# Taking the parts of a projected half right behind its last product, in a Performer-attention kernel on one core

## Chip, cores and metric

The kernel runs on 1 core of one Trainium2 chip. The metric is the device time of one launch in microseconds. The kernel before took 1294.76 us (median of 3 runs, 1294.49 to 1295.84).

## The reference, cut to what matters

The input x is 8 batches x 1024 tokens x 512 features. Per batch there are 16 heads of 32 features and 128 random features.

```python
def feature_map(x, orf):
    proj = x @ orf.T / d_k ** 0.25
    norm = jnp.sum(x * x, axis=-1, keepdims=True) / (2.0 * math.sqrt(d_k))
    return (jnp.exp(proj - norm) + EPS) / math.sqrt(m)
q = feature_map(split(x @ Wq.T + bq), orf)
k = feature_map(split(x @ Wk.T + bk), orf)
v = split(x @ Wv.T + bv)
kv = jnp.einsum('nlm,nld->nmd', k, v)
ksum = jnp.sum(k, axis=1)
out = jnp.einsum('nlm,nmd->nld', q, concat(kv, ksum))
out = out[..., :-1] / out[..., -1:]          # then @ Wo.T + bo
x = layernorm(x + attention(x))
x = layernorm(x + x @ (ternary(weight) * scale).T)
```

## The kernel before, in words

One core works through the 8 batches in order. The 16 heads are taken as 4 groups of 4. Each group has two *units*, an even one for its keys and an odd one for its queries, so a batch has units 0 to 7, and behind them an output stage (projection, layer norm, ternary product, layer norm).

A matrix product with full precision is made of three products of rounded parts: high x high, low x high, high x low. So each projected tile must be split into a high part (rounded copy), a low part (the rest) and, for the norm, a square.

All work is one list, `SCHEDULE`, of small stages. Every engine walks through the same list and does its own share of each stage, in order, with semaphores between the engines. So a stage's place in the list sets, on every engine by itself, what it is queued behind. `unit_stages` (L72) writes the list of a unit. A stage is a tuple of a letter, the batch, the unit and a piece:

- **P** (PE, L951): six products of 128x512 into one PSUM bank, half of one projected half of a unit. A unit has two halves, each of twelve products, (P, half, 0) and (P, half, 1). In unit u the list holds what belongs to unit u+2 (`two`) and the first part of unit u+3 (`three`): `p[0]` is the second part of half 0 of u+2, with its last product; `p[1]` and `p[2]` are half 1 of u+2; `p[3]` is the first part of half 0 of u+3.
- **S** (`s0`, `s1`; ACT, L649 and L651): the high part and the square of a half, both read from PSUM. **L** (`l0`, `l1`; DVE, L816): the low part, which reads PSUM and waits for both of ACT's. Projections have PSUM banks 0 and 1, taken in turn, and a bank is free again when L has read it; PE waits for that before it starts a P in it.
- **Q** (`q0`, `q1`; DVE, L824 and L828): the squares are transposed and summed. **N** (DVE, L834 to L839): the norms. **LIFT** and **NL** (DMAs of the SP and POOL queues): high, low and norms are copied to the stacked operand of the features of unit u+2.
- **F** (0 to 7; PE, L964 for keys and L969 for queries; ACT, L668): the features of unit u, a tile of 128x512 each. PE's product goes to one of three banks, ACT takes the exponential. In a key unit DVE adds the tiles up: tile 1 is added to tile 0 (L777), tiles 2 to 7 one after the other to the total (L780). These are seven additions, called a1 to a7 here.
- **G** (0 to 7; PE, L982): keys times values. Behind tile 7 the total of the additions is multiplied by ones (L991), which waits for a7. G belongs to a group's query unit and stands behind its F 0 and 1. ACT copies the result (L673 to L680).
- **KVT** (PE, L999 and L1000; DVE, L842): the result transposed. **GG** 0 and 1 (PE, L1014): query features times it; it waits for DVE's copy and for the features of its half, and DVE then transposes, sums and inverts the denominators (L850 to L855). **R** 0 and 1 (DVE, L865 and L867): the division.
- **WF** (DVE, L755 and L756): a quarter of the ternary weights, once in the launch, in batch 0.

The waits that the prediction speaks of:

```python
if old is not None:                                   # PE: the bank's last reader
    pe.wait_ge(*old_bank(old))                        # for P: v_plo, counted by L
pe.wait_ge(v_ks.sem, v_ks.nth(b, 7 * u + 7))          # PE, G of tile 7: a7
pe.wait_ge(v_kvc.sem, v_kvc.nth(b, g + 1))            # PE, GG 0: DVE's copy L842
dve.wait_ge(a_p.sem, a_p.nth(b, 2 * (2 * u + h) + 2)) # DVE, L: high part and square
dve.wait_ge(v_ks.sem, v_ks.nth(b, 7 * g + r - 1))     # DVE, L780: the addition before
```

Of the kernel before, what the change touches and what calls it, by code (L numbers as in the profile page):

```python
# [49 lines left out]
NU = 2 * NG  # L50
# [12 lines left out]
def split_at(b, g):  # L63

    return 4 if sums_on_pe(b, g) else 0


def is_key(u):
    return u % 2 == 0


def unit_stages(b, u):  # L72

    g = u // 2

    def later(k):
        n = NU * b + u + k
        return (n // NU, n % NU) if n < NU * B else None

    def project(unit, h, part):  # L80
        return [("P", *unit, h, part)] if unit else []

    def take(kind, unit, h):
        return [(kind, *unit, h)] if unit else []

    def f(*tiles):
        return [("F", b, u, n) for n in tiles]

    def xt(*tiles):
        return [("XT", b + 1, t) for t in tiles] if b + 1 < B else []  # L90

    two, three = later(2), later(3)
    p = [project(two, 0, 1), project(two, 1, 0), project(two, 1, 1), project(three, 0, 0)]
    s0, s1, l0, l1, q0, q1 = (take(kind, two, h) for kind in "SLQ" for h in range(2))
    norm = [("N", *two)] if two else []
    lift = [("LIFT", *two), ("NL", *two)] if two else []
    if is_key(u):
        st = [[("ST", b - 1, t)] if u == 0 and b else [] for t in (TT - 2, TT - 1)]
        half = [("G", b, g, r) for r in range(split_at(b, g))]
        early = [("AG", b, 0, 0), ("AG", b, 1, 0)] if b + 1 == B and u + 2 == NU else []  # L100
        if u == 0:
            seq = f(0, 1) + p[1] + s0 + l0 + f(2, 3) + q0 + st[0] + p[2] + f(4, 5) + half + s1 + l1 + f(6, 7) + q1 + norm + lift
            seq += st[1] + p[3]
        else:
            seq = f(0, 1) + p[0] + f(2, 3) + p[1] + s0 + l0 + f(4, 5) + q0 + half + p[2] + early + f(6, 7) + s1 + l1 + q1 + norm + lift + p[3]
        if u == 0 and b == 0:
            seq += [("WA", 0, k) for k in range(KT)]
        if u == 2 and b == 0:
            seq += [("WF", 0, 1)]
        if u == 2 and 0 < b < B - 1:  # L110
            seq += [("LX", b + 1, t) for t in range(5)]
        return seq
    kv = [("G", b, g, r) for r in range(split_at(b, g), 8)]
    if u < NU - 1:
        seq = p[0] + f(0, 1)
        if u == 1 and b == 0:
            seq += [("WS", 0)]
        if b + 1 == B and u == NU - 3:
            seq += p[1] + s0 + l0 + kv + f(2, 3) + p[2] + f(4, 5) + s1 + q0 + [("KVT", b, g)] + f(6, 7) + l1 + [("GG", b, g, 0)] + q1 + norm + lift
            seq += [("GG", b, g, 1), ("R", b, g, 0)] + [("LR", b, t) for t in range(4)]  # L120
        elif u < NU - 3:
            seq += kv + f(2, 3) + p[1] + [("KVT", b, g)] + s0 + l0 + f(4, 5) + p[2] + f(6, 7) + s1 + q0 + [("GG", b, g, 0)]
            seq += l1 + p[3] + [("R", b, g, 0), ("GG", b, g, 1)] + q1 + norm + lift
        else:
            seq += xt(0) + kv + f(2, 3) + p[1] + [("KVT", b, g)] + s0 + l0 + xt(1, 2) + f(4, 5) + xt(3)
            seq += [("LX", b + 1, t) for t in range(5, TT)] + p[2] + [("GG", b, g, 0), ("R", b, g, 0)] + q0
            seq += s1 + xt(4) + f(6, 7) + xt(5) + l1 + p[3] + xt(6, 7) + [("GG", b, g, 1)] + q1 + norm + lift
            seq += [("LR", b, t) for t in range(4)]
        seq += [("R", b, g, 1)] if b + 1 < B or u < NU - 3 else []
        if u == 1 and b == 0:  # L130
            seq += [("WF", 0, 0)]
        if u == 3 and b == 0:
            seq.insert(seq.index(("L", 0, 5, 0)) + 1, ("WF", 0, 2))
            seq += [("WF", 0, 3)] + [("LX", 1, t) for t in range(5)]
        return seq
    if b + 1 == B:
        seq = [("R", b, g - 1, 1), ("AG", b, 2, 0)] + f(0, 1, 2) + kv + [("AG", b, 0, 1)] + f(3) + [("OK", b, 0, 0)]
        seq += [("KVT", b, g)] + f(4, 5) + [("AG", b, 1, 1), ("AG", b, 2, 1), ("A", b, 0), ("A", b, 1), ("OK", b, 0, 1), ("OK", b, 0, 2)]
        seq += [("GG", b, g, 0), ("R", b, g, 0, 0), ("AG", b, g, 0, 0)] + f(6, 7) + [("OK", b, 1, k) for k in range(3)]
        seq += [("R", b, g, 0, 1), ("AG", b, g, 0, 1), ("OK", b, 0, 3), ("LN", b, 0), ("OK", b, 1, 3), ("LN", b, 1), ("A", b, 2), ("A", b, 3)]  # L140
        seq += [("GG", b, g, 1)] + [("OK", b, 2, k) for k in range(KT)] + [("LN", b, 2), ("Y", b, 0), ("A", b, 4)]
        return seq + [("LR", b, t) for t in range(4, TT)]
    v0 = [("V", b + 1, 0)] if two else []
    seq = p[0] + f(0, 1) + kv + f(2, 3) + p[1] + [("KVT", b, g)] + s0 + l0 + f(4, 5) + [("GG", b, g, 0)] + q0 + [("R", b, g, 0, 0)]
    seq += p[2] + f(6, 7) + s1 + l1 + [("A", b, 0), ("A", b, 1)] + v0 + [("R", b, g, 0, 1), ("GG", b, g, 1)]
    return seq + [("LR", b, t) for t in range(4, TT)]
# [55 lines left out]
for _b in range(B):  # L202
    for _u in range(NU):
        SCHEDULE += unit_stages(_b, _u)
    SCHEDULE += output_stages(_b)
# [879 lines left out]
```

## Time and profile before

| | |
|---|---|
| median of the runs | 1294.76 us |
| profiled execution, its own time | 1293.62 us |
| its span, first to last instruction | 1291.8 us |
| PE busy | 1262.5 us (98%) |
| PE weight load busy | 958.8 us (74%) |
| DVE busy | 940.8 us (73%) |
| ACT busy | 700.6 us (54%) |
| POOL busy | 326.6 us (25%) |

Busy time is the union of the instructions of an engine; matmuls overlap in the record, so a busy PE is not PE at its peak. The granted TensorE clock was 0.999 over the span.

### The profile page before, as it was taken

To read this page: it belongs to the slowest core of one execution; us is meant where nothing else is said; L and a number is where in the kernel's file an instruction comes from. 1 tells how busy PE (TensorE), PEld (TensorE's weight loads), DVE (VectorE), ACT (ScalarE), POOL (GpSimd) and SP (SyncE) were. 2 spreads that over 40 slices of the span, in tenths; PEclk is the share of its full clock that TensorE was granted. 3 is DMA by queue.
4 is the path that set the end of the run, shared out by engine and by line. 5 is a ranking of instruction groups with operands and counts; after the bars stand their busy time and mean duration, and the time that the engine had idled before them with its cause. 6 is when DMAs were issued, how large, how long until landed. Compare 5 with 4: busy or idle time off the path is not lost.

```text
span 1291.8 us, 24909 instructions
## 1 busy us (share of the span) xinstructions
PE 1262.5 (98%) x8626; PEld 958.8 (74%) x8626; DVE 940.8 (73%) x1775; ACT 700.6 (54%) x1403; POOL 326.6 (25%) x617
## 2 busy tenths in 40 slices
PE   9999999999999999999999999999999999999986
PEld 8767788677877678776787768876788767886665
DVE  6588765887658875788757886588865787657766
ACT  5557435574356743567336663367534665446534
POOL 0102342024310243103431034211252022420043
PEclk9999999999999999999999999999999999999999
DMA  6658404783146821567215762258612685036611
GB/s 236 153 125 220 100 33 121 171 195 88 52 110 174 201 61 58 129 171 187 62 58 130 181 169 65 65 132 209 153 44 71 152 208 142 33 87 144 149 58 65
DMA packets 82749, 160.33 MB, mean 124 GB/s; under 512 B 17856, under 2 KB 36416, under 8 KB 82112
## 3 DMA queue, kind: packets, MB, share of 16 engines
q1 hardware_dynamic: 68880, 139.78, 43.4%
q10 hardware_dynamic: 9648, 16.85, 3.4%
q0 software_dynamic: 4096, 2.11, 0.7%
q8 instruction: 69, 1.13, 0.4%
q14 instruction: 56, 0.46, 0.1%
HBM read 39.13 MB, written 16.78 MB: 43 GB/s over the span
## 4 chain that ended last, share of the span: by engine, by line
PE 76%; DVE 10%; issue 5%; ACT 4%; POOL 0%; ACTq 0%; DVEq 0%; POOLq 0%
PE ps L951 21%; PE ps L914 18%; PE ps L1014 7%; PE ps L964 6%; PE ps L982 5%; PE ps L937 4%; PE ps L939 4%; PE ps L938 4%; PE ps L969 4%; PE ps L1040 2%; ACT features L668 1%; DVE squares_turned L824 1%; DVE den L865 1%; DVE unit_lo L816 1%; DVE dens_turned L850 1%
## 5 line engine op out<-in xcount | busy, mean ns | idle before, releaser
L668 ACT ACTIVATE features<-ps 128x512 f32<-128x512 f32 x512 | 278.7, 604 | 248.2 <-PE ps L964 168.8
L570 POOL DMA_DIRECT2D stacks<-norm_rows x128 | 69.5, 546 | 530.4 <-DVE norm_rows L839 256.8
L964 PEld LDWEIGHTS ps<-orf_stack,stacks 98*128 98x128 f32 x1024 | 130.9, 192 | 28.0 <-issue 20.3
L914 PE MATMUL ps<-Wo_hi,stacks 128*128 128x512 f32 x448 | 150.5, 402 | 0.0
L641 ACT ACTIVATE values_then_attention<-ps 128x512 f32<-128x512 f32 x64 | 38.2, 597 | 196.9 <-PE ps L939 193.8
L780 DVE TENSOR_TENSOR den<-den,features 128x512 f32<-128x512 f32 x186 | 128.1, 689 | 12.9
L964 PE MATMUL ps<-orf_stack,stacks 98*128 98x128 f32 x1024 | 130.5, 272 | 0.0
L1014 PE MATMUL ps<-features,kv_ksum 128*32 128x512 f32 x1024 | 123.1, 598 | 3.3 <-ACT features L668 2.1
L816 DVE SCALAR_TENSOR_TENSOR unit_lo<-ps,cols,unit_hi 128x512 fp32r<-128x512 f32 x128 | 94.3, 736 | 39.0 <-ACT squares L651 39.0
L550 POOL TENSOR_SCALAR stats<-stats 128x1 f32<-128x1 f32 x128 | 36.0, 282 | 334.9 <-DVE stats L767 334.8
L914 PE MATMUL ps<-W_ternary,stacks 128*128 128x512 f32 x448 | 110.7, 389 | 0.0
L951 PE MATMUL ps<-x_hi,Wq_hi 128*128 128x512 f32 x256 | 103.5, 404 | 6.5 <-DVE unit_lo L816 6.5
L951 PE MATMUL ps<-x_hi,Wk_hi 128*128 128x512 f32 x256 | 108.5, 424 | 1.3 <-DVE x_lo L809 1.3
L937 PE MATMUL ps<-Wv_hi,x_hi 128*128 128x512 f32 x256 | 102.6, 401 | 0.8
L616 ACT ACTIVATE rows<-rows,stats 128x512 f32<-128x512 f32 x112 | 88.3, 815 | 26.4 <-POOL stats L554 25.6
L914 PEld LDWEIGHTS ps<-Wo_hi,stacks 128*128 128x128 f32 x448 | 84.2, 188 | 24.3 <-issue 7.1
L951 PE MATMUL ps<-x_lo,Wq_hi 128*128 128x512 f32 x256 | 101.1, 395 | 0.0
L951 PE MATMUL ps<-x_lo,Wk_hi 128*128 128x512 f32 x256 | 100.8, 394 | 0.0
L951 PE MATMUL ps<-x_hi,Wq_lo 128*128 128x512 f32 x256 | 100.6, 393 | 0.0
L951 PE MATMUL ps<-x_hi,Wk_lo 128*128 128x512 f32 x256 | 100.2, 391 | 0.0
L939 PE MATMUL ps<-Wv_hi,x_lo 128*128 128x512 f32 x256 | 100.0, 391 | 0.0
L938 PE MATMUL ps<-Wv_lo,x_hi 128*128 128x512 f32 x256 | 100.0, 390 | 0.0
(132 smaller groups left out, 2528.0 us busy)
## 6 DMA issues: line engine op xcount, KB each, us to landing
stacks<-unit_hi SPq DMA_DIRECT2D x512, 128.0 KB, 2.4
stacks<-unit_lo SPq DMA_DIRECT2D x256, 128.0 KB, 2.8
out<-rows ACTq DMA_DIRECT2D x56, 256.0 KB, 2.0
rows<-in_x_t SPq DMA_DIRECT2D x49, 256.0 KB, 3.4
rows<-in_x SPq DMA_DIRECT2D x32, 256.0 KB, 3.8
features<-in_x SPq DMA_DIRECT2D x32, 256.0 KB, 4.1
values_then_attention<-in_x_t SPq DMA_DIRECT2D x8, 256.0 KB, 7.4
stacks<-norm_rows POOLq DMA_DIRECT2D x128, 16.0 KB, 2.7
```

The costliest lines, as they stand in the source:

```text
L570: pool.dma_start(slot[row:row + 1, :].rearrange("o (t c) -> o t c", c=DH), NN[:, u % 2, part, :].bitcast(F32)).then_inc(n_lifted[u % 2].se ...
L616: nc.scalar.activation(row, row, ACT.Identity, scale=ln(k, t, 10), bias=ln(k, t, 11))\
L668: nc.scalar.activation(FE[:, n % 8, :, 0:M], ps[:, :].rearrange("p (a m) -> p a m", a=HG), ACT.Exp, scale=C_EXP).then_inc(a_exp.sem, 1)
L780: ins = nc.vector.tensor_tensor(total, total, FE[:, r, :, 0:M], ALU.add)
L816: nc.vector.scalar_tensor_tensor(out=EL[:, u % 2, half], in0=ps[:, :], scalar=BC[:, u:u + 1], in1=EH[:, u % 2, half].bitcast(F32), op0=ALU ...
L914: last = mm(out, a, b, start=(n == 0), stop=(n == len(terms) - 1))
L937: mm(ps[:, :], XH[:, k, c], WH["v"][:, k, :], start=(k == 0), stop=False)
L938: mm(ps[:, :], XH[:, k, c], WL["v"][:, k, :], start=False, stop=False)
L939: last = mm(ps[:, :], XL[:, k, c], WH["v"][:, k, :], start=False, stop=(k == KT - 1))
L951: last = mm(ps[:, :], *terms[n], start=(n == 0), stop=(n == len(terms) - 1))
L964: last = mm(ps[:, M * h:M * (h + 1)], slot[0:QK, L * h + P * r:L * h + P * (r + 1)], ORF[0:QK, h, :], start=True, stop=True)
L1014: last = mm(bank[DH * h:DH * (h + 1), :], KVS[:, g % 2, c + DH * h:c + DH * (h + 1)], FE[:, HG * half + h, :, 0:M], start=True, stop=True, ...
```

## The change

The lists of the key units 2, 4 and 6 and of the query units 1 and 3 are put in another order. Units 0, 5 and 7 and the output stage keep theirs. No instruction is added, removed or resized.

```diff
@@ key units 2, 4, 6
-            seq = f(0, 1) + p[0] + f(2, 3) + p[1] + s0 + l0 + f(4, 5) + q0 + half + p[2] + early + f(6, 7) + s1 + l1 + q1 + norm + lift + p[3]
+            seq = f(0, 1) + p[0] + s0 + l0 + f(2, 3) + p[1] + q0 + f(4, 5) + half + p[2] + early + s1 + l1 + f(6, 7) + q1 + norm + lift + p[3]
@@ query units 1, 3 (NU is 8)
-        seq = p[0] + f(0, 1)
+        seq = p[0] + (s0 + l0 if u < NU - 3 else []) + f(0, 1)
         if u == 1 and b == 0:
             seq += [("WS", 0)]
@@
         elif u < NU - 3:
-            seq += kv + f(2, 3) + p[1] + [("KVT", b, g)] + s0 + l0 + f(4, 5) + p[2] + f(6, 7) + s1 + q0 + [("GG", b, g, 0)]
-            seq += l1 + p[3] + [("R", b, g, 0), ("GG", b, g, 1)] + q1 + norm + lift
+            seq += kv + f(2, 3) + p[1] + [("KVT", b, g)] + q0 + f(4, 5) + p[2] + s1 + l1 + f(6, 7) + [("GG", b, g, 0)]
+            seq += p[3] + q1 + [("GG", b, g, 1)] + norm + lift + [("R", b, g, 0)]
```

In unit 3 of batch 0 a quarter of the ternary weights (WF) stands directly behind `l0` and moves with it.

## Rows read from the trace of the kernel before

**Rows 1.** The page: busy time, share of span and instructions of each engine.

```profile
PE 1262.5 (98%) x8626; PEld 958.8 (74%) x8626; DVE 940.8 (73%) x1775; ACT 700.6 (54%) x1403; POOL 326.6 (25%) x617
```

**Rows 2.** Waits, PE's weight load: waiter <- awaited: us in total, times, longest.

```profile
PEld ps L951 <- DVE unit_lo L816: 8.2, 10, 1.8
```

**Rows 3.** Timeline, batch 1, units 4, 6: start, length, instruction, count [idle before <-releaser].

```profile
260.56 1.01 PE L964 MATMUL ps<-orf_stack,stacks 98*128 98x128 f32 x8
261.41 0.46 PE L951 MATMUL ps<-x_hi,Wq_hi 128*128 128x512 f32 x1
...
284.54 1.01 PE L964 MATMUL ps<-orf_stack,stacks 98*128 98x128 f32 x8
285.99 0.50 PE L951 MATMUL ps<-x_hi,Wq_hi 128*128 128x512 f32 x1 [0.44 <-DVE unit_lo L816]
```

**Rows 4.** Timeline of DVE, batch 1, key unit 6, from its first addition.

```profile
283.00 0.68 DVE L777 TENSOR_TENSOR den<-features 128x512 f32<-128x512 f32 x1
283.79 1.49 DVE L780 TENSOR_TENSOR den<-den,features 128x512 f32<-128x512 f32 x2
285.19 0.75 DVE L816 SCALAR_TENSOR_TENSOR unit_lo<-ps,cols,unit_hi 128x512 fp32r<-128x512 f32 x1
285.85 1.48 DVE L780 TENSOR_TENSOR den<-den,features 128x512 f32<-128x512 f32 x2
287.25 0.70 DVE L824 STREAM_TRANSPOSE squares_turned<-squares 128x512 f32<-128x512 f32 x1
...
288.59 1.48 DVE L780 TENSOR_TENSOR den<-den,features 128x512 f32<-128x512 f32 x2
```

**Rows 5.** Timeline of ACT, batch 1, key unit 6: the square of half 0.

```profile
282.12 0.70 ACT L651 ACTIVATE squares<-ps,cols 128x512 f32<-128x512 f32 x1
```

**Rows 6.** Timeline of PE's weight load, batch 1: ones times total, units 3 and 7.

```profile
243.28 0.24 PEld L991 LDWEIGHTS ps<-den,ones 128*32 128x32 f32 x8
...
291.09 0.24 PEld L991 LDWEIGHTS ps<-den,ones 128*32 128x32 f32 x8
```

**Rows 7.** Timeline of DVE, batch 1, key unit 2: the last two additions.

```profile
240.74 1.48 DVE L780 TENSOR_TENSOR den<-den,features 128x512 f32<-128x512 f32 x2
```

**Rows 8.** Timeline of DVE, batch 1, end of unit 3 and the first addition behind.

```profile
254.76 0.25 DVE L855 RECIPROCAL cols<-cols 128x16 f32<-128x16 f32 x1
...
256.33 0.21 DVE L834 STREAM_TRANSPOSE norms_turned<-cols 128x32 f32<-128x32 f32 x1
...
256.91 0.70 DVE L865 STREAM_TRANSPOSE den<-cols 128x512 f32<-128x512 f32 x1
...
258.38 0.68 DVE L777 TENSOR_TENSOR den<-features 128x512 f32<-128x512 f32 x1
```

**Rows 9.** Timelines of DVE and PE, batch 7: first addition of unit 4, then unit 5.

```profile
1200.65 0.68 DVE L777 TENSOR_TENSOR den<-features 128x512 f32<-128x512 f32 x1
...
1206.47 0.63 PE L969 MATMUL ps<-stacks,orf_stack 98*128 98x512 f32 x2
1208.43 0.50 PE L951 MATMUL ps<-x_hi,Wq_hi 128*128 128x512 f32 x1 [1.33 <-DVE unit_lo L816]
```

**Rows 10.** Timelines of DVE, PE and weight load, batch 0, units 2 to 5.

```profile
86.59 0.48 DVE L755 TENSOR_SCALAR W_ternary<-rows,cols 128x512 fp32r<-128x512 f32 x1
...
87.84 0.43 DVE L842 COPY kv_ksum<-ps 128x256 f32<-128x256 f32 x1
...
90.05 1.92 PE L1014 MATMUL ps<-features,kv_ksum 128*32 128x512 f32 x16
...
101.32 0.68 DVE L777 TENSOR_TENSOR den<-features 128x512 f32<-128x512 f32 x1
...
109.41 0.24 PEld L991 LDWEIGHTS ps<-den,ones 128*32 128x32 f32 x8
```

**Rows 11.** Timelines of ACT and PE, batch 1, unit 3: features 4 to 7, GG 1.

```profile
247.11 2.18 ACT L668 ACTIVATE features<-ps 128x512 f32<-128x512 f32 x4
...
251.78 1.92 PE L1014 MATMUL ps<-features,kv_ksum 128*32 128x512 f32 x16
```

## The prediction, made before the changed kernel was run

> **What bounds the kernel now.** I read the page's busy line first. PE is busy for 98% of the span and DVE for 73% [rows 1], so almost all the time is PE's own work, and the change does not touch that: P, F, G, KVT and GG stand in the same order before and after on PE, with the same banks. So the change can only pay where PE waits, and the next view is the waits. PE's weight load waited 8.2 us in ten places for the low part L816 [rows 2]. That is the one wait for the moved work, and since each wait is counted once there, 8.2 us is the ceiling of the gain.
>
> Third, the timeline at such a place. Seven of the ten are alike: unit 6 of batches 0 to 6. Behind features 6 and 7, p3 needs the PSUM bank that l0 frees. In unit 4 of batch 1 PE goes from the eight feature products to p3 in 0.85 us (260.56 to 261.41), in unit 6 in 1.45 us (284.54 to 285.99) [rows 3]: 0.60 us lost, seven times. DVE shows why. It comes late to unit 6: its first addition a1 starts at 283.00, and l0 stands behind a1, a2 and a3, ending at 285.19 + 0.75 = 285.94 [rows 4]; PE goes on 0.05 us later [rows 3]. The data for l0 had long been there: the square that it waits for ended at 282.82 [rows 5]. The eighth is in batch 7, 1.33 us at 1208.43 [rows 9], and the other two in batch 0, in units 2 and 4, where ternary weights delay DVE. In the key units 2 and 4 of the other batches PE does not wait for L at all.
>
> **DVE's new order in a key unit.** Before, it ran a1 a2 a3 L0 a4 a5 Q0 a6 a7 L1 Q1 N, after, a1 L0 a2 a3 Q0 a4 a5 L1 a6 a7 Q1 N. The distances from start to start come from unit 6 [rows 4]. Addition to addition is 0.79 (283.00 to 283.79); the second of that pair starts at 284.58, so addition to L is 0.61; L to addition 0.66; the addition before Q0 starts at 285.85 + 0.79 = 286.64, so addition to Q is 0.61; both instructions of Q take 1.34 (287.25 to 288.59). An addition directly behind another costs 0.13 to 0.18 more than any other pair, since it waits for the first one's result.
>
> With these, L0 starts 0.61 behind a1 instead of 2.19. L1 starts at 0.61 + 0.66 + 0.79 + 0.61 + 1.34 + 0.79 + 0.61 = 5.41 behind a1. a7 starts at 5.41 + 0.66 + 0.79 = 6.86, where it was at 6.38 (288.59 + 0.79): the last addition comes 0.48 us *later*, since L1 now stands ahead of it. Q1 and N come 0.18 earlier, for one chained pair of additions fewer.
>
> L0 will not wait for ACT: even at its old place the square is done at 282.82 [rows 5], before a1 ends at 283.68 [rows 4], and it only moves forward.
>
> **What is late next: the product of ones with the total (L991).** It waits for a7. In batch 1, a7 of unit 6 ends at 288.59 + 1.48 = 290.07 [rows 4] and L991's weights load at 291.09 [rows 6]. After the change a7 ends at 290.55 and PE may go on at 290.60. PE, without its 0.60, would be there at 290.49. So a new wait of 0.11 us takes part of the gain: 0.49 us is left per unit 6, times 7, 3.43 us. The first addition of unit 6 stays where it is, as unit 5 keeps its order, and DVE's end of unit 4 does not get later.
>
> Rule against row: the trace has a price between DVE instructions that depends on what follows what, 0.79 against 0.61 [rows 4]. The Trainium skill ("VectorE: DVE Perf Modes", section "The TRN2 errata") says that an exposed memory latency between instructions is a fixed cost of each one. By that rule alone the order would not change the sum of the distances, and a7 would be late by a whole instruction, an estimate of about 0.69 us in place of 0.48. The new wait would be 0.32 us, the gain per unit 6 0.28, and the total about 3.5 us, 1291.3 us. I go by the rows, and keep this inside the range.
>
> **The same shift in units 2 and 4, batches 1 to 7.** Here there is nothing to gain (but for batch 7), and the question is whether the later a7 makes a wait. a7 of unit 2 ends at 240.74 + 1.48 = 242.22 [rows 7]; L991 loads at 243.28 [rows 6], so 1.01 us are free, with the 0.05 above. The shift is 0.48 and what comes in from the query unit ahead. That unit's end on DVE: the reciprocal of GG 1, Q1, N, then R1, then a1. Q1 now stands ahead of GG 1, R0 behind N. Taken out: 1.57 (254.76 to 256.33), of which the reciprocal's 0.25 stays; put in: one R, 1.47 (256.91 to 258.38) [rows 8]. So a1 comes 0.15 later. 0.48 + 0.15 = 0.63 is under 1.01: cost nothing; the cover left is 0.38 us, in 13 places (units 2 and 4 of batches 1 to 7, without unit 4 of batch 7, where PE is late anyway).
>
> **Batch 7, unit 5.** Its own order is unchanged, but its half-1 projection needs the bank that L1 of unit 4 frees. It starts at 1208.43 after 1.33 us idle; its features are done at 1206.47 + 0.63 = 1207.10 [rows 9]. After: a1 at 1200.65 + 0.15, L1 5.41 behind, so it ends at 1206.96, freed at 1207.01. All of the 1.33 us is gained. Everything behind it hangs on PE's products and moves along.
>
> **Batch 0.** In unit 2 the wait of over 1 us for l0 goes, but DVE's total is what binds there. In unit 3 l0 and a quarter of the ternary weights now stand ahead of the copy L842 that GG 0 waits for. The copy started at 87.84, behind another such quarter, which took 1.25 (86.59 to 87.84) [rows 10]. It now also has L0 (0.66) and this 1.25 ahead of it, and gains 0.03 from the order above: it ends at 87.84 + 1.88 + 0.43 = 90.15, and GG 0 starts at 90.20 instead of 90.05 [rows 10]. So unit 3 ends 0.15 later than before. In unit 4, a1 was at 101.32, now 0.15 + 0.15 later; a7 is ready 6.86 + 0.69 + 0.05 behind, at 109.22, and L991 loaded at 109.41 [rows 10]. Of the waits in batch 0, 8.2 - 7 x 0.60 - 1.33 = 2.7 us in units 2, 4 and what the weight load adds, only 0.2 us is kept.
>
> **ACT and the queues.** S now stands ahead of two exponentials, which come later by at most both of its instructions, an estimate of 1.3 us from the rows of 0.70. The tightest reader is GG 1 in query units: feature 7 was ready at 247.11 + 2.18 = 249.29 and GG 1 starts at 251.78 [rows 11]: 2.49 us of cover. In the projection-bound stretches features are paced by PE, with three banks; I cost this at nothing, and at 1.3 us less cover it still holds. LIFT waits for L1, so SP's DMAs (and x loads queued behind them) start earlier, never later; N is not later in key units, so neither are POOL's norm copies. R0's later end is read only by the next group.
>
> **Sum.** 3.43 + 1.33 + 0.2 = 4.96 us. The profiled execution took 1293.62 us, so it would be 1288.7. The median of the runs is 1.14 us above the profiled one; taken from the median, 1294.76 - 4.96 = 1289.8 us, 0.38% faster.
>
> **Rivals.** *A, full gain:* a7 is early enough or PE is covered elsewhere, all 8.2 us go: 1286.6 us. Against it: a7 in unit 6 has 0.97 us of cover today and loses 0.48 + 0.60. Chance 0.07.
>
> *B, taken back:* a7's shift is 0.97 or more instead of 0.48, so in unit 6 PE waits at L991 for all that it saved at p3. Only batch 7 is left: 1294.76 - 1.33 = 1293.4, no measurable change. For it: DVE is the engine that is late in unit 6, and a reordering takes no work from it. Against: the distances of rows 4 were measured at these very pairs. Chance 0.14.
>
> *C, slower:* L0 in key units stalls DVE, in order, for ACT's square, as L816 does in query units; every addition stands behind it. From a shift of 0.86 on (1.01 - 0.15), L991 waits in the 13 places too. With a stall of 0.75, an instruction's length, the shift is 1.23: 13 x 0.37 = 4.8 us, unit 6 loses 0.26 x 7 = 1.8, batch 7 still gains 0.6: 1300.8 us. For it: S0 too stands in a queue, ahead of it two exponentials. Against: rows 5, by 0.86 us even at the old place. Chance 0.07.
>
> *D, the diff does more than its title:* R0 also goes behind GG 1, Q1 and N, in 16 query units. Were its reader waiting, each would pay up to the 1.47 of an R. Its only readers are the next group's G and DVE itself, priced above at 0.15. No separate time: it would show as B.
>
> **Chances.** Forecast with its own range (1288.0 to 1291.8): 0.70; A 0.07; B 0.14; C 0.07; anything else 0.02. A measurement of this kernel can tell about 0.2%, 2.6 us, from no change, so faster means under 1292.2. Faster: the forecast, A and a little of B, 0.79. Same 0.13, slower 0.08. The range goes from A's side, 1286.8, to short of B, 1292.8.
>
> **What would show it.** In the waits after, L951 <- L816 should be gone or under 0.5 us, with a new entry L991 <- DVE den L780 of about 0.1 us in unit 7 of seven batches and 0.3 to 0.9 us in units 3 and 5 of batch 0, and L1014 <- L842 longer once in batch 0. DVE's timeline in unit 6: L816 0.61 behind L777, the last addition's end 7.55 behind a1's start. It is wrong if L991 waits in units 3 and 5 of batch 1, or if L816 shows idle time before it in key units.

## The result, and the profile after

The changed kernel took 1287.72 us (median of 4 runs, 1287.18 to 1288.69) against 1294.72 us: ratio 0.9945, 95% interval 0.9934 to 0.9957, so 7.0 us faster. The forecast was 1289.8 us with the range 1286.8 to 1292.8. The direction and the mechanism held; the gain was 2 us larger than the 4.96 us of the sum. By the time alone the result lies nearer to rival A (1286.6) than to the forecast; what separates the two is the traces below.

The profiled execution took 1287.18 us, its span 1285.35 us, 6.4 us less than before. The page's line of busy times, beside [rows 1]:

```profile
PE 1262.2 (98%) x8626; PEld 956.9 (74%) x8626; DVE 937.2 (73%) x1775; ACT 703.2 (55%) x1403; POOL 327.8 (26%) x617
```

PE's busy time is the same to 0.3 us: what went is idle time. The waits of PE after (waiter <- awaited: us in total, times, longest), with all entries of 0.4 us or more that changed by more than 0.1 us, and the one for features:

```profile
PE ps L1040 <- ACT values_then_attention L616: 3.7, 3, 2.1
PE ps L1014 <- ACT features L668: 2.1, 7, 0.3
...
PE ps L969 <- ACT features L668: 1.1, 1, 1.1
...
PE ps L991 <- DVE den L780: 0.7, 2, 0.4
PE ps L914 <- DVE x_lo L892: 0.4, 2, 0.3
PE ps L1014 <- DVE kv_ksum L842: 0.4, 1, 0.4
```

Before, the same view of PE began with these two lines, the first of which has no counterpart after:

```profile
PE ps L951 <- DVE unit_lo L816: 6.5, 10, 1.3
PE ps L1040 <- ACT values_then_attention L616: 5.2, 4, 2.1
```

In the place of the first stand two entries that were not there: L991 <- L780 (twice, 0.7 us) and L1014 <- L842 (once, 0.4 us). These three waits are in batch 0. The 1.5 us less at L1040 are one wait in the last batch that PE reached late, after a stretch at half clock, 1.2 GHz (last section); they are no gain of the change, and in its second trace the line is back at 5.2. The entry that I had based the ceiling on, PE's *weight load* waiting for L816 [rows 2], did not shrink but grew, from 8.2 us:

```profile
PEld ps L951 <- DVE unit_lo L816: 12.7, 16, 0.8
```

That is idle time of the weight load while PE is still busy with the products before; it says nothing of lost time. The row to go by was PE's own.

Unit 6 of batch 1 on DVE after, beside [rows 4], then PE at p3 and at L991, beside [rows 3, 6] (timelines: start, length, instruction, count):

```profile
280.90 0.68 DVE L777 TENSOR_TENSOR den<-features 128x512 f32<-128x512 f32 x1
281.50 0.74 DVE L816 SCALAR_TENSOR_TENSOR unit_lo<-ps,cols,unit_hi 128x512 fp32r<-128x512 f32 x1
282.16 1.48 DVE L780 TENSOR_TENSOR den<-den,features 128x512 f32<-128x512 f32 x2
283.56 0.70 DVE L824 STREAM_TRANSPOSE squares_turned<-squares 128x512 f32<-128x512 f32 x1
...
284.90 1.48 DVE L780 TENSOR_TENSOR den<-den,features 128x512 f32<-128x512 f32 x2
286.30 0.75 DVE L816 SCALAR_TENSOR_TENSOR unit_lo<-ps,cols,unit_hi 128x512 fp32r<-128x512 f32 x1
286.96 1.48 DVE L780 TENSOR_TENSOR den<-den,features 128x512 f32<-128x512 f32 x2
```

```profile
282.46 1.00 PE L964 MATMUL ps<-orf_stack,stacks 98*128 98x128 f32 x8
283.31 0.45 PE L951 MATMUL ps<-x_hi,Wq_hi 128*128 128x512 f32 x1
...
288.49 0.42 PE L991 MATMUL ps<-den,ones 128*32 128x128 f32 x8
```

```profile
288.49 0.16 PEld L991 LDWEIGHTS ps<-den,ones 128*32 128x32 f32 x8
```

L0 starts 0.60 behind a1, L1 5.40, and the last addition ends at 286.96 + 1.48 = 288.44, 7.54 behind a1's start: forecast 0.61, 5.41 and 7.55. PE goes from features to p3 in 0.85 us, as in the units that never waited. At L991 the weights now load at 288.49, together with the product, where they were 0.11 us ahead of it.

**Where the time went.** I took the start of the first feature product (L964 or L969) of every unit from the traces and compared them. The numbers are us, changed minus before; "step" is what is gained (-) or lost (+) since the row above.

| start of | before | after | difference | step |
|---|---|---|---|---|
| batch 0, unit 0 | 47.78 | 47.06 | -0.71 | -0.71 |
| batch 0, unit 3 | 82.76 | 80.87 | -1.89 | -1.17 |
| batch 0, unit 4 | 95.36 | 94.44 | -0.92 | +0.98 |
| batch 0, unit 5 | 107.17 | 105.08 | -2.09 | -1.18 |
| batch 0, unit 6 | 120.56 | 119.05 | -1.51 | +0.58 |
| batch 7, unit 5 | 1206.47 | 1200.77 | -5.71 | -4.20 |
| batch 7, unit 6 | 1220.37 | 1213.08 | -7.29 | -1.59 |
| batch 7, unit 7 | 1227.37 | 1220.52 | -6.85 | +0.45 |
| end | 1291.78 | 1285.35 | -6.43 | +0.42 |

The 4.20 us are seven steps of 0.62 to 0.69 between the starts of units 6 and 7 of batches 0 to 6, less 0.03 to 0.09 up to the start of the following batch. From batch 0, unit 0 to batch 7, unit 6 ("the middle" from here on) the gain is 6.58 us. The first 0.71 us precede any reordered stage, and the last 0.87 us are given back; the experiments show what these are.

### The profile page after: what moved, and what is told of

Read it like the earlier page. It is cut to its first block, busy times and chain, and to the rows that moved or that the text cites. A ratio compares the mean times of both kernels' runs of the same rounds, so it can differ in the third digit from the quotient of the medians.

```text
span 1285.3 us, 24909 instructions
## 1 busy us (share of the span) xinstructions
PE 1262.2 (98%) x8626; PEld 956.9 (74%) x8626; DVE 937.2 (73%) x1775; ACT 703.2 (55%) x1403; POOL 327.8 (26%) x617
## 3 DMA queue, kind: packets, MB, share of 16 engines
q0 software_dynamic: 4096, 2.11, 0.7%
## 4 chain that ended last, share of the span: by engine, by line
PE 82%; ACT 5%; DVE 5%; issue 3%; POOL 0%; ACTq 0%; DVEq 0%; POOLq 0%
PE ps L951 24%; PE ps L914 19%; PE ps L964 8%; PE ps L1014 8%; PE ps L982 4%; PE ps L937 4%; PE ps L939 4%; PE ps L938 4%; PE ps L969 4%; PE ps L1040 2%; ACT features L668 2%; ACT x_hi L636 1%; PE ps L991 1%; DVE squares_turned L824 1%; DVE den L780 1%
## 5 line engine op out<-in xcount | busy, mean ns | idle before, releaser
L668 ACT ACTIVATE features<-ps 128x512 f32<-128x512 f32 x512 | 279.0, 605 | 183.9 <-PE ps L964 128.3
L964 PEld LDWEIGHTS ps<-orf_stack,stacks 98*128 98x128 f32 x1024 | 130.8, 191 | 28.1 <-issue 20.3
L780 DVE TENSOR_TENSOR den<-den,features 128x512 f32<-128x512 f32 x186 | 127.9, 688 | 10.8 <-DVE den L780 0.5
L964 PE MATMUL ps<-orf_stack,stacks 98*128 98x128 f32 x1024 | 130.4, 272 | 0.0
L816 DVE SCALAR_TENSOR_TENSOR unit_lo<-ps,cols,unit_hi 128x512 fp32r<-128x512 f32 x128 | 95.6, 747 | 46.2 <-ACT squares L651 46.2
L1014 PE MATMUL ps<-features,kv_ksum 128*32 128x512 f32 x1024 | 123.1, 598 | 3.7 <-ACT features L668 2.1
L649 ACT ACTIVATE unit_hi<-ps,cols 128x512 fp32r<-128x512 f32 x128 | 88.9, 694 | 66.5 <-PE ps L951 66.5
```

Of the source, the lines that this page charges most:

```text
L649: nc.scalar.activation(EH[:, u % 2, half], ps[:, :], ACT.Identity, bias=BC[:, u:u + 1]).then_inc(a_p.sem, 1)
L668: nc.scalar.activation(FE[:, n % 8, :, 0:M], ps[:, :].rearrange("p (a m) -> p a m", a=HG), ACT.Exp, scale=C_EXP).then_inc(a_exp.sem, 1)
L780: ins = nc.vector.tensor_tensor(total, total, FE[:, r, :, 0:M], ALU.add)
L816: nc.vector.scalar_tensor_tensor(out=EL[:, u % 2, half], in0=ps[:, :], scalar=BC[:, u:u + 1], in1=EH[:, u % 2, half].bitcast(F32), op0=ALU ...
L964: last = mm(ps[:, M * h:M * (h + 1)], slot[0:QK, L * h + P * r:L * h + P * (r + 1)], ORF[0:QK, h, :], start=True, stop=True)
L1014: last = mm(bank[DH * h:DH * (h + 1), :], KVS[:, g % 2, c + DH * h:c + DH * (h + 1)], FE[:, HG * half + h, :, 0:M], start=True, stop=True, ...
```

## Experiments

Every kernel below ran beside the kernel before on the same chip. The first four runs share one chip, the next three another, the last four a third. The medians of the kernel before there were 1294.27, 1295.17 and 1294.48 us. Trace figures are differences to the first trace of the kernel before.

**Unit 6 alone.** The new order of key units only where u is 6, everything else as before.

```diff
-            seq = <old order of key units>
+            seq = (<new order>) if u == 6 else (<old order>)
```

> Only key unit 6 has the new order, in all batches; units 1 to 4 are as before. Theory (seven waits of 0.60 us for l0 in unit 6 go, and almost nothing takes their place): 7 x 0.60 = 4.2 us faster than before, in the trace 0.60 us per batch between the start of unit 6 and the start of unit 7, nothing in any other unit. Rival (the later a7 takes back part, as I forecast blind): 3.4 us. Second rival (the gain comes from all units, through fewer waits on ACT): under 2 us.

Measured: 1289.69 us, ratio 0.9964 (0.9951 to 0.9977), 4.6 us. In the trace the seven steps at unit 6 are 0.62 to 0.67, and from the start of unit 0 of batch 0 to that of unit 5 of batch 7 it gains 4.02 us. PE still has the other three waits:

```profile
PE ps L951 <- DVE unit_lo L816: 3.2, 3, 1.3
```

So about two thirds of the gain are this one wait, and next to nothing of it is taken back: the theory's 4.2 us fit, the blind 3.4 are too small.

**All but unit 6.** The mirror image: the change, with unit 6 in its old order.

```diff
-            seq = <new order of key units>
+            seq = (<new order>) if u < 6 else (<old order>)
```

> The change in units 1 to 4, unit 6 in its old order. Theory: the seven waits of 0.60 us stay, batch 0 gains 0.8 us and unit 5 of batch 7 1.6 us, of which 0.9 us is given back towards the end: 1.5 to 2.4 us faster than before. With the first run the two parts should sum to the gain of the whole change. Rival (the parts interact, units 2 to 4 help unit 6): more than 3 us.

Measured: 1292.32 us, ratio 0.999 (0.998 to 1.0). The median is 1.95 us below that of the kernel before; the ratio alone would say 1.3 us, since it goes by means and two of the twelve executions took 1296.66 and 1298.3 us. The seven waits are there, 2.9 us in PE's view:

```profile
PE ps L951 <- DVE unit_lo L816: 2.9, 7, 0.4
```

In the trace batch 0 gains 0.83 us up to unit 6, batches 1 to 6 nothing (the difference stays between -0.40 and -0.55), and unit 5 of batch 7 1.60 us. The two halves of the change sum to 4.02 + 0.83 + 1.60 = 6.45 us in the traces, against 6.58 for both together: they do not interact. By the medians the sum is 1.95 + 4.58 = 6.5 us against 7.0 for the whole, within these intervals. This trace gives back 1.6 us behind unit 6 of batch 7, more than any other of these four: PE ran at half clock for a stretch of that unit (granted clock 0.61 from 1222 to 1226 us, products of L982 and L985 about 0.43 us apart from group to group instead of 0.22 in the first experiment).

**First half only.** In key units only s0 and l0 move up, q0, s1 and l1 stay.

```diff
-            seq = ... + p[1] + q0 + f(4, 5) + half + p[2] + early + s1 + l1 + f(6, 7) + q1 + ...
+            seq = ... + p[1] + f(4, 5) + q0 + half + p[2] + early + f(6, 7) + s1 + l1 + q1 + ...
```

> Key units 2, 4 and 6: only the first half's parts (s0, l0) move up; q0, s1, l1 are at their old places. Query units as in the change. Theory: unit 6 still gains 0.60 us per batch, since l0 is what p3 waits for, and the last addition stays 6.38 us behind the first, so no wait at the product of ones in unit 7. But in batch 7 l1 of unit 4 is late again, and the wait of about 1.4 us at the start of unit 5 is back: 1.0 to 1.6 us slower than the whole change. Rival (moving the second half is what matters in unit 6): the 0.60 us waits are back.

Measured: 1288.13 us, ratio 0.9956 (0.9945 to 0.9968). Unit 6 gains its 0.62 to 0.66 us in batches 0 to 6, so it is l0 that counts there. In batch 0, 0.10 us is lost in unit 5 instead of 0.58, and 1.16 in unit 3 instead of 0.98. And the wait at the start of unit 5 of batch 7 is back, as in [rows 9]:

```profile
1202.96 0.50 PE L951 MATMUL ps<-x_hi,Wq_hi 128*128 128x512 f32 x1 [1.32 <-DVE unit_lo L816]
```

Moving the second half pays in one place in the launch, and costs in another. The middle gains 5.58 us, 1.0 less than with the whole change, where 1.0 to 1.6 was expected; the timed difference to the change (0.9956 against 0.9945) is too small for its intervals, the trace decides here.

**The ternary quarter behind the copy.**

```diff
-            seq.insert(seq.index(("L", 0, 5, 0)) + 1, ("WF", 0, 2))
+            seq.insert(seq.index(("KVT", 0, 1)) + 1, ("WF", 0, 2))
```

> As the change, but the quarter of the ternary weights in unit 3 of batch 0 stands behind DVE's copy L842 again. The wait of 0.39 us of GG 0 for the copy goes. Theory (DVE's total binds batch 0 from unit 2 to unit 5): the 0.4 us come back as a longer wait for the last addition at L991 in unit 5, and the start of unit 6 of batch 0 stays within 0.1 us. Rival (PE's own waits add up): it comes 0.4 us earlier.

Measured: 1286.51 us, ratio 0.9942 (0.993 to 0.9954). My theory fell. The step at the start of unit 4 is +0.52 instead of +0.98, the one at unit 6 is +0.56 as in the change, so 0.46 us are really gained (in the middle 7.08 us against 6.58). What DVE did at the end of unit 3 explains it, in the change and then here:

```profile
94.58 0.72 DVE L850 STREAM_TRANSPOSE dens_turned<-ps 128x512 f32<-128x512 f32 x1 [0.91 <-PE ps L1014]
```

```profile
94.81 0.72 DVE L850 STREAM_TRANSPOSE dens_turned<-ps 128x512 f32<-128x512 f32 x1 [0.60 <-PE ps L1014]
```

DVE itself waits there, for GG 1. DVE is late in the key unit and idle at the end of the query unit, so a delay of PE in between goes straight through to the next unit.

**The changed kernel again.** No edit.

> The changed kernel unaltered, to see what of the differences is not the change's. Theory: the first 0.7 us (start of unit 0 of batch 0, ahead of any reordered stage), the 0.45 us given back at the start of unit 7 of batch 7 and the 0.42 us given back in the last 10 us vary from one execution to the next. Rival: all three are there again to 0.1 us, so they belong to the change.

Measured: 1287.82 us, ratio 0.9943 (0.993 to 0.9955). The start of unit 0 of batch 0 is +0.55 against before, not -0.71; over all traces it lies between -0.71 and +0.63 with no edit that could touch it. In the middle the gain is 6.60 us (6.58 in the first trace). Behind it the steps are +0.19 and +0.07 instead of +0.45 and +0.42. So the beginning and the end vary with the execution, and the middle of the changed kernel hardly does. (Of the kernel before, a second trace follows below.)

**Squares too.** In key units 2 and 4, q1 also goes ahead of features 6 and 7, so that the last addition comes another 1.34 us later.

```diff
-            seq = <new order of key units>
+            seq = (... + s1 + l1 + q1 + f(6, 7) + norm + lift + p[3]) if u < 6 else (<new order>)
```

> As the change, but in key units 2 and 4 q1 also stands ahead of the features 6 and 7, so the last addition comes another 1.34 us later (1.82 us later than before). It measures the point from which a later last addition costs. The cover at the product of ones was 1.17 us in batch 1, unit 3 (last addition's end at 242.22, product at 243.39). Theory: each of 13 places in batches 1 to 7 waits 1.82 - 1.12 = 0.7 us, 9 us slower than the change, and about 1.3 us more in each of the two places of batch 0: 10 to 12 us slower. Rival (the cover is larger, as three banks and eight feature tiles let PE run on): under 3 us slower.

Measured: 1301.21 us, ratio 1.0048 (1.0035 to 1.006): 13.4 us slower than the changed kernel beside it, and slower than before. That is beyond the 10 to 12 us expected. PE's waits begin with

```profile
PE ps L991 <- DVE den L780: 11.2, 15, 1.7
```

and in unit 3 of batch 1 DVE's last additions and PE's product read

```profile
244.68 1.48 DVE L780 TENSOR_TENSOR den<-den,features 128x512 f32<-128x512 f32 x2
...
246.22 0.42 PE L991 MATMUL ps<-den,ones 128*32 128x128 f32 x8 [0.57 <-DVE den L780]
```

The product starts 0.06 us behind the last addition. Against the changed kernel, eleven of the 13 places cost 0.72 or 0.73 us, the other two 1.07, and batch 0's two 2.5 and 1.3 us: 13.9 us. Of the 2.5 us, 1.34 are the longer wait. Behind it PE ran at half clock for a stretch (granted clock 0.68 from 88 to 92 us), which it did in no other trace there; that is the rest, and most of what the expectation missed. Why two places cost 1.07 is open. With the shift of 1.82 the cover before was 1.82 - 0.73 = 1.09 us; from the rows it is 243.39 (the product's start, 0.11 behind its weights) - 242.22 - 0.06 = 1.11 [rows 6, 7]. A wait at L991 once the last addition is late enough is the slower rival's mechanism, and this shows from what shift it costs; its other half, DVE stalling for ACT's square, was seen in no run. The experiment's own rival, a larger cover, is out.

**Rows of x held back.** The loads of x rows in batch 7 wait for the first feature product of unit 7.

```diff
-                        wait(d_st[t].sem, d_st[t].nth(b, 0))
+                        wait(d_st[t].sem, d_st[t].nth(b, 0)); t or wait(t_f.sem, t_f.nth(b, 8 * NU - 7))
```

> As the change, but the loads of four rows tiles of x in batch 7, issued right behind the copies to the stack of unit 7, wait until unit 7's first features are done. Theory (these loads share the DMA engines with the last low-part copy, which landed 4.4 us behind its issue where others take 2.6 to 2.9): the copy lands in about 3 us and unit 7 of batch 7 starts 1 us earlier against unit 6; the end may still be held by the later loads. Rival (the landing time is not due to the loads): unit 7 starts where it does in the change.

Measured: 1286.73 us, ratio 0.9938 (0.9924 to 0.9951). Unit 7 of batch 7 starts 0.84 us nearer to unit 6 than before, and the last low-part copy landed 2.78 us behind its issue. That looked like the theory, but the first four kernels, with the loads unmoved, had landings of 2.7 to 3.1 us too. So I ran both again on one chip, with the kernel before.

**Before, changed and held once more.** Three runs, without a new edit.

> The kernel before, unaltered, for a second trace of it. Theory: between the start of unit 0 of batch 0 and the start of unit 5 of batch 7 it agrees with the first trace to 0.2 us; the start of unit 0 and the start of unit 7 of batch 7 may differ by up to 1 us. Rival (the seven waits of 0.60 us were a feature of one execution): they are not there, or not 0.6 us.

> The changed kernel unaltered, beside the next run on one chip. Theory (the loads of x rows slow the last low-part copy on chips where they collide): the copy lands 4 us or more behind its issue, if the kernel before does so too in this call. Rival (its landing time varies by itself): 2.7 to 3.1 us in one of the two.

> The change with the loads of x rows held until unit 7's first features, once more, with the changed kernel beside it. Theory: the copy lands within 2.8 us whatever it does in the other two, unit 7 starts 0.85 us earlier if they have the long landing, and 0.4 us of that is left at the end. Rival: landing as in the changed kernel.

Measured: before 1294.33 us (0.9999, 0.999 to 1.0008), changed 1287.26 us (0.995, 0.9938 to 0.9963), held 1287.26 us (0.9946, 0.9932 to 0.9959). The kernel before has its ten waits again, 6.3 us, and its seven units 6 are as long as in its first trace to 0.02 us; the theory's 0.2 us was too narrow for the whole, since it drifted by 0.6 us over the middle against its first trace, in steps of 0.05 or less. So the gain in the middle is 6.5 to 6.6 us against the one trace of the kernel before and 7.1 to 7.2 against the other, and the medians' 7.0 lies between. The changed kernel gained 6.48 us in the middle here. The last low-part copy of batch 7 landed 2.75 us behind its issue in the unchanged order and 2.78 with the loads held.

**Combined.** The ternary quarter behind the copy, only the first half moved up in batch 0, loads held.

> The change with three things: the ternary quarter behind the copy, only the first half moved up in batch 0 (where the second half costs a wait of 0.48 us in unit 5 and gains nothing), and the loads of rows held. Theory: 0.46 + 0.48 us from batch 0 and up to 0.4 us from the loads, 0.9 to 1.3 us faster than the changed kernel. Rival (DVE binds in batch 0): within 0.3 us of the run with held loads.

Measured: 1286.63 us, ratio 0.9938 (0.9926 to 0.9951); timed, it cannot be told from the changed kernel beside it. In the trace it gains 7.72 us in the middle, 1.1 to 1.2 us more than the change, as expected: the steps of batch 0 are +0.41 and +0.11 instead of +0.98 and +0.58. But its last copy landed in 4.28 us, with the loads held. That ends the theory of the loads: the landing time varies with the execution.

| execution | copy's landing, us behind issue | landing to unit 7's first product, us |
|---|---|---|
| before, before again | 4.00, 4.61 | 0.09, 0.09 |
| changed, again, third | 4.42, 4.20, 2.75 | 0.09, 0.09, 0.49 |
| loads held, again, combined | 2.78, 2.78, 4.28 | 0.48, 0.46, 0.09 |
| the first four, squares too | 2.82, 2.72, 2.84, 3.14, 4.32 | 0.43, 2.11, 0.39, 0.12, 0.09 |

Where the landing takes over 4 us, PE starts 0.09 us behind it, so the copy is what it waits for, although the trace's waits name ACT (L969 <- L668, 1.1 us). The 2.11 us are the run with all but unit 6, whose unit 6 ran partly at half clock.

## Why the prediction was right, and where it was off

- *What bounds the kernel* was right: the order on PE is the same, PE's busy time changed by 0.3 us, and ten waits for L816 went. ACT, which I costed at nothing, cost nothing that shows: L1014 waits for features 2.1 us in seven places before and after.
- *DVE's new order* was right to 0.01 us in its distances, and L0 waits for nothing in unit 6 (0.60 behind a1). The dependence of the distance on what follows what was real: by the rule of the Trainium skill ("VectorE: DVE Perf Modes", "The TRN2 errata"), a fixed cost of each instruction, taken alone, the last addition would have ended an estimated 0.2 us later than it did.
- *Unit 6* was mis-sized in both its terms. I took 0.60 us as lost and a new wait of 0.11 us off it. From the start of unit 6 to that of unit 7 the change gains 0.62 to 0.69, since the first product behind a stall is slow too: the next one started 0.33 us behind it before (285.99 to 286.32) and starts 0.29 behind it now (283.31 to 283.60). And L991 takes back less than 0.11: I let it be bound by its weights' load, 0.11 us ahead of the product, but the product started with the weights (both at 288.49), 0.05 us behind the last addition. From the last product ahead of L991 to the first one behind it, PE takes 0.46 to 0.52 us in the seven batches instead of 0.42. Measured 0.60 kept per batch against 0.49: 4.20 us against 3.43.
- *Batch 7, unit 5*: 1.33 forecast, 1.59 measured. I counted PE's idle time. From the first feature product to the projection it is 1.96 us before (1206.47 to 1208.43) and 0.47 after (1200.77 to 1201.24), which gives 1.49; the other 0.1 us is the slow first product behind a stall (0.50 us long instead of 0.39 in [rows 9] and after).
- *Batch 0*: 0.2 forecast, 0.80 measured; this is the term that was furthest off, in proportion. I let a1 come 0.15 us later per query unit. It came no later: between GG 1's transpose (L850) and the end of the last R, what left the chain (Q1, 1.41 us, and 0.06 us of N, which is slower behind Q1) is as long as the R that entered it (1.47). The two rows before, then the two after:

```profile
71.09 0.72 DVE L850 STREAM_TRANSPOSE dens_turned<-ps 128x512 f32<-128x512 f32 x1
75.70 0.51 DVE L755 TENSOR_SCALAR W_ternary<-rows,cols 128x512 fp32r<-128x512 f32 x1
```

```profile
70.37 0.72 DVE L850 STREAM_TRANSPOSE dens_turned<-ps 128x512 f32<-128x512 f32 x1 [0.91 <-PE ps L1014]
74.98 0.48 DVE L755 TENSOR_SCALAR W_ternary<-rows,cols 128x512 fp32r<-128x512 f32 x1
```

  Both are 4.61 us apart, and in batch 1, from L850 to a1, it is 4.61 before and after too. The 0.15 stood in the forecast twice, and both ternary quarters ahead of the copy took 1.18 us instead of 1.25. So a1 of unit 4, which I had 0.30 us later, came 0.23 earlier (100.38 against 101.32, less the 0.71 us of the beginning), and L991 was again counted from its weights, 0.11 us ahead of the product that in fact started with them. Together that is the 0.6 us. PE still waits at all three places that I named:

```profile
83.76 0.43 PE L991 MATMUL ps<-den,ones 128*32 128x128 f32 x8 [0.36 <-DVE den L780]
...
89.15 0.64 PE L1014 MATMUL ps<-features,kv_ksum 128*32 128x512 f32 x4 [0.39 <-DVE kv_ksum L842]
```

- *The sum*: 0.77 + 0.26 + 0.60 explain the step from 4.96 to the 6.6 us of the middle. The rest to the 7.0 us of the medians is within their intervals. All three terms were too small, so the errors added up; that the time still lies well inside the range is owed to a range that went 3 us to either side.
- *Units 2 and 4 of the other batches* were right: no wait at L991, and the run with the squares moved shows 1.1 us of cover where I had computed 1.01 from the weights. The shift to be covered was 0.48, not 0.63, as a1 came no later.
- *What would show it*: L991's 0.1 us in unit 7 did not appear in the waits (it is 0.04 to 0.10 us of slower products instead); the rest did. But PE's weight load does wait 12.7 us for L816 after, and [rows 2] was the wrong row for the ceiling. PE's 6.5 us, plus the slow first products, was the right one.
- *Rivals*: taken back (B) is out, the steps of unit 6 are whole; slower (C) needs a shift above 1.1 us and got 0.48. The full gain (A) is not reached: batch 0 gives up 0.8 us and still waits 1.1 at three places. But in unit 6 A was close to true, and its 8.2 us came from the wrong row. The later R0 (D) cost nothing, by the same 4.61 us.

## What to carry to other kernels

Where an in-order engine is late, move the piece that frees another engine's buffer ahead of the work that nobody waits for yet, and then price the piece that you pushed back by its own reader's cover: here 0.48 us against 1.1 us, where 1.82 us cost 13 us. Take a ceiling from the idle time of the engine that bounds the kernel, not from its weight loads. Compare two traces by the starts of the same product in each stage; it tells a gain of 0.6 us per batch from the microsecond or so by which beginnings and ends vary. Have a second trace of the kernel before as well: here two of them drift apart by 0.6 us in small steps, which is a tenth of the gain.

## What the runs showed of the hardware that I had not expected

- Weights that load late cost less here than the 0.11 us by which they otherwise load ahead. In unit 7 of batch 1 the operand of L991 came so late that its weights loaded together with the product instead of 0.11 us ahead. From the last product before to the first behind, PE lost 0.04 us (0.46 against 0.42), in the other batches up to 0.10.
- The same copy (the last low part of batch 7) landed 2.75, 4.20 and 4.42 us behind its issue in three executions of one kernel, the last two on different chips. Holding other loads back did not settle it (2.78, 2.78, 4.28). What sets it is open.
- In some executions the granted clock was halved for a stretch in the last batch. In the first trace of the changed kernel, the stretch 1270 to 1274 had a mean of 0.57, and its products of 512 columns were 0.43 us apart:

```profile
1266.00:1270.00 4.00, 2.04 (x10) 1.36 (x8) 3.64 (x8) 2.22 (x3) 2.09 (x6) 1.00 0.10 36
1270.00:1274.00 4.00, 3.89 (x12) 2.83 (x12) 1.11 (x3) 2.23 (x3) 1.04 (x3) 0.57 0.18 67
```

(Columns: stretch, us, busy us of PE, weight load, DVE, ACT and POOL, granted clock, DMA share, GB/s.) Here PE had been busy for 2.04 of the 4 us before. In the second execution the same products came behind the same pause at full clock, 0.23 us apart:

```profile
1268.00:1272.00 4.00, 1.94 (x11) 1.42 (x10) 3.21 (x7) 1.85 (x3) 2.09 (x7) 1.00 0.17 66
1272.00:1276.00 4.00, 2.48 (x13) 1.81 (x12) 2.32 (x4) 2.23 (x4) 1.17 (x4) 1.00 0.17 66
```

The mean of 0.57 is mostly the lower of the two levels, 1.2 GHz. This is the 0.42 us lost at the end of the first trace (0.07 in the second). It is not the change's: the second trace of the kernel before has such a stretch at the same place and the first has none there, and from the start of unit 7 to the end they took 64.87 and 64.41 us (64.83 and 64.48 for the changed kernel with and without; the copy landed late in all four). In the combined kernel a second such stretch lay at 1218.5 to 1222 (0.79 in the mean), in unit 7 of batch 7, and this last part took 66.3 us instead of 64.4 to 65.3.
